# Graph maxima on one core: node positions by a TensorE product, the end mask in the comparison, one register load per group

## The reference

```python
ew = 1.0 / (pos[src] - pos[dst])
def _graph_conv(x, src, dst, ew, W_rel, b_rel, W_root):
    msg = x[src] * ew[:, None]
    agg = jax.ops.segment_max(msg, dst, num_segments=N)
    agg = jnp.where(jnp.isfinite(agg), agg, 0.0)
    return agg @ W_rel.T + b_rel + x @ W_root.T
```

## Time and profile before

| | us |
|---|---|
| median of 3 runs | 5897.64 (5895.26 to 5898.86) |
| profiled execution | 5895.44 |
| its span | 5893.6 |
| preparation (0 to about 191) | 191 |
| maxima stage (about 191 to 1540) | 1349 |

### The profile page before, as it was taken

One profiled execution on the slowest core, in us unless ns is written; L12 is line 12 of the kernel. 1 busy time (PEld: TensorE's weight loads), 2 busy tenths in 40 slices (PEclk: granted clock), 3 DMA queues, 4 the chain that ended last, 5 costly groups with the idle time before them and its releaser, 6 DMA issues. The chain is left out here.

```text
span 5893.6 us, 89741 instructions
## 1 busy us (share of the span) xinstructions
PE 4011.4 (68%) x17170; PEld 2633.9 (45%) x17171; DVE 3584.3 (61%) x11586; ACT 1285.5 (22%) x3616; POOL 2887.2 (49%) x2883
## 2 busy tenths in 40 slices
PE   0466666666577777674997995889998883555531
PEld 0355555555333333332554663555555552444421
DVE  5788888888655655654333115545454546888846
ACT  0243334343222222220000001222222221000020
POOL 1566666666277777772000000577777771333300
PEclk9755555555677777776998996555555555999955
DMA  6466666666312111123886661566666663555520
GB/s 130 148 195 194 195 196 199 200 199 195 103 58 59 51 59 59 51 59 81 200 199 178 193 206 42 157 176 176 176 177 176 176 173 59 142 142 143 142 76 22
DMA packets 1037793, 820.28 MB, mean 139 GB/s; under 512 B 539459, under 2 KB 945586, under 8 KB 1024056
## 3 DMA queue, kind: packets, MB, share of 16 engines
q1 hardware_dynamic: 787472, 600.56, 34.3%
q0 software_dynamic: 98672, 176.74, 11.8%
q10 hardware_dynamic: 151592, 42.33, 3.4%
HBM read 578.48 MB, written 167.05 MB: 126 GB/s over the span
## 5 line engine op out<-in xcount | busy, mean ns | idle before, releaser
L2087 POOL DMA_INDIRECT ring<-xl_rows,idx x896 | 892.5, 996 | 1283.7 <-DVE idx L2166 1009.0
L378 POOL DMA_INDIRECT ringa<-x_sign_pos,idxa x880 | 890.2, 1012 | 434.5 <-issue 275.5
L964 POOL DMA_INDIRECT edge_counts<-cntb,placeb x850 | 844.0, 993 | 349.6 <-issue 257.0
L2159 PE MATMUL zps<-We,eaT 64*128 64x128 f32 x1792 | 710.8, 498 | 0.0
L440 PE MATMUL sela<-hota,endsa 128*128 128x128 f32 x1760 | 404.0, 401 | 335.9 <-ACT endsa L405 314.4
L2157 PE MATMUL zps<-xr,hotT 128*128 x2688 | 454.0, 301 | 145.0 <-ACT hotT L2139 78.4
L2513 PE MATMUL ops<-val,hot 128*128 128x200 f32 x1792 | 364.1, 347 | 263.1 <-DVE out L2532 165.3
L440 PEld LDWEIGHTS sela<-hota,endsa 128*128 128x128 f32 x1760 | 346.2, 293 | 417.2 <-DVE acc L500 318.1
L2189 DVE TENSOR_TENSOR z<-zps,ring 128x512 f32<-128x512 f32 x224 | 154.9, 691 | 604.2 <-PE zps L2159 513.9
L2159 PEld LDWEIGHTS zps<-We,eaT 64*128 64x128 f32 x1792 | 447.3, 309 | 164.6 <-issue 148.2
L2480 POOL TENSOR_TENSOR val<-rows,val 128x512 f32<-128x512 f32 x224 | 235.3, 1050 | 493.4 <-ACT val L2499 493.4
(11 more groups left out here) (337 smaller groups left out, 6245.1 us busy)
## 6 DMA issues: line engine op xcount, KB each, us to landing
edge_counts<-zeroa SPq DMA_DIRECT2D x55, 1568.0 KB
matd<-edge_counts SPq DMA_DIRECT2D x12, 6272.0 KB
posb<-edge_keys SPq DMA_DIRECT2D x50, 1216.0 KB
dstb<-dst_in_tile SPq DMA_DIRECT2D x112, 512.0 KB
xl_of_steps<-ring SPq DMA_DIRECT2D x224, 256.0 KB
rows<-xl_of_steps SPq DMA_DIRECT2D x224, 256.0 KB
reseta<-resets SPq DMA_DIRECT2D x110, 512.0 KB
eaT<-in_eaT SPq DMA_DIRECT2D x896, 32.0 KB
```

What stands on the lines that cost most here:

```text
L378: p.indirect_dma_start(out=ring[:, k, :], out_offset=None, in_=table, in_offset=bass.IndirectOffsetOnAxis(ap=idx[:, k:k + 1], axis=0)).the ...
L964: p.indirect_dma_start(out=g.M.rearrange("d s -> (d s)").unsqueeze(1), out_offset=bass.IndirectOffsetOnAxis(ap=place[:, i, k:k + 1], axis= ...
L2087: p.indirect_dma_start(out=ring[:, c, k, :], out_offset=None, in_=g.xl_rows[0:N, :], in_offset=bass.IndirectOffsetOnAxis(ap=idx[:, q * GS ...
L2159: ins = t.matmul(zk, eaT[:, c, k, :], g.We[:, :], start=False, stop=True)
```

## The change

Four edits, all for `max_pass`.

The positions of the destinations no longer come from four DVE instructions. ACT builds the transposed one-hot matrix `hotT` (nodes on the partitions, edges along the columns) from a bf16 broadcast of the destinations, in two instructions per group, and TensorE multiplies it by the positions of the node tile, split into three bf16 parts, four products of three columns. DVE adds the three parts by one small reduction. `g.posb` goes; `pos3` takes its place. ACT issues the loads of the broadcast row, half a turn at a time.

`g.dend` is the destination where the edge is the last of its destination, and -1 elsewhere; `hot` compares with it, so `ends` is copied without a mask, by one instruction.

DVE loads the node tiles of a group once, after the scan, for the adds of the next step. TensorE has a load of its own. The four adds of DVE now stand together at the start of its step.

`prepare` makes the new tables, and writes the bf16 row to DRAM.

```diff
@@ prepare
+        drel_h = m.sb("drel_h", [P, KB, P], BF16)
+        pos = m.sb("pos_of_nodes", [P, NT])
...
-                s.wait_ge(s_v, V_T + 8)
+                s.wait_ge(s_v, V_T + 13)
...
+                for dst, srct in ((g.d0row, flag[:, :, :]), (g.drelrow, drel_r[:, :, :]), (g.drelhalf, drel_h[:, :, :]),
+                                  (g.srcrow, rows_f[:, :, 0, :])):
...
-                s.dma_start(g.posb[:, 0:N], a["node_vec"].partition_broadcast(P)).then_inc(s_pos, 16)
+                s.dma_start(pos[:, 0:NT - 1], a["node_vec"][0:(NT - 1) * P].rearrange("(t p) -> p t", p=P)).then_inc(s_nodes, 16)
+                s.dma_start(pos[0:N - (NT - 1) * P, NT - 1:NT], a["node_vec"][(NT - 1) * P:N].unsqueeze(1)).then_inc(s_nodes, 16)
...
+                link(v.tensor_copy(drel_h[:, :, :], drel_r[:, :, :]))
+                v.wait_ge(s_nodes, 32)
+                link(v.tensor_copy(g.pos3[:, :, 0], pos[:, :]))
+                link(v.tensor_tensor(pos_rest[:, :], pos[:, :], g.pos3[:, :, 0], ALU.subtract))
+                link(v.tensor_copy(g.pos3[:, :, 1], pos_rest[:, :]))
+                link(v.tensor_tensor(g.pos3[:, :, 2], pos_rest[:, :], g.pos3[:, :, 1], ALU.subtract))
...
+                link(v.scalar_tensor_tensor(out=g.dend[:, :], in0=g.drel[:, :], scalar=1.0, in1=g.endf[:, :],
+                                            op0=ALU.add, op1=ALU.mult))
+                link(v.tensor_scalar(g.dend[:, :], g.dend[:, :], 1.0, None, ALU.subtract))
@@ max_pass, ACT
-                    for k in range(GS):
-                        ins = s.activation(ends[:, q % 2, k, :], runT[q % 2][:, k * P:(k + 1) * P], ACT.Copy,
-                                           scale=g.endf[:, bass.ds(G * GS + k, 1)])
-                    ins.then_inc(s_e, 1)
+                    s.activation(ends[:, q % 2, :, :].rearrange("p k f -> p (k f)"), runT[q % 2][:, :], ACT.Copy
+                                 ).then_inc(s_e, 1)
+
+                def load(turn, h):
+
+                    s.dma_start(dstb[:, h, :], g.drelhalfflat[bass.ds(turn * (U * P) + h * (U * P // 2), U * P // 2)
+                                                              ].partition_broadcast(P)).then_inc(s_b[h], 16)
+
+                def places(turn, G, q):
+
+                    h, off = q // 2, (q % 2) * GS * P
+                    if q % 2 == 0:
+                        s.wait_ge(s_b[h], 16 * (turn + 1))
+                    wait(s, s_hotT, G)
+                    s.activation(apart[:, :], dstb[:, h, off:off + GS * P], ACT.Abs, bias=nodes[:, :]).then_inc(s_apart, 1)
+                    wait(s, s_at, G - 1)
+                    wait(s, s_apart, G + 1)
+                    if q % 2 == 1:
+                        load(turn + 1, h)
+                    s.activation(hotT[:, q % 2, :], apart[:, :], ACT.Relu, scale=-1.0, bias=1.0).then_inc(s_hotT, 1)
...
                 def body(it):
                     for q in range(NG):
                         G = it * NG + q
+                        places(it if q < NG - 1 else it + 1, G + 1, (q + 1) % NG)
@@ max_pass, TensorE
+                def positions(G, q):
+                    t.load(regs, g.T[0:1, bass.ds(G * GS, GS)])
+                    T = [t.snap(r, min_val=0, max_val=NT - 1) for r in regs]
+                    wait(t, s_hotT, G + 1)
+                    wait(t, s_c, (G - 2) * NCH + 1)
+                    for k in range(GS):
+                        ins = t.matmul(where[q % 2][:, 3 * k:3 * k + 3], hotT[:, q % 2, k * P:(k + 1) * P],
+                                       g.pos3.rearrange("p t i -> p (t i)")[:, bass.ds(T[k] * 3, 3)], start=True, stop=True)
+                    ins.then_inc(s_at, 1)
+
                 def body(it):
                     for q in range(NG):
                         G = it * NG + q
+                        positions(G, q)
                         for lag, stage in ((3, select), (1, transposed), (2, back)):
@@ max_pass, DVE step
                     if adds:
-                        A = tiles_of(G - 4, aregs)
-                        add(*at(4), 0, A)
+                        A = [v.snap(r, min_val=0, max_val=NT - 1) for r in aregs]
+                        for k in range(GS):
+                            add(*at(4), k, A)
                     if new:
 
                         wait(v, s_sel, G - NG + 1)
 
                         v.tensor_tensor(hot[:, q, :, :], bc_mid(g.iota_n[:, :], GS),
-                                        bc_last(g.drel[:, bass.ds(G * GS, GS)], P), ALU.is_equal).then_inc(s_hot, 1)
-                        T = tiles_of(G, tregs)
-                        dst_position(G, 0, T)
...
-                        dst_position(G, 3, T)
+                                        bc_last(g.dend[:, bass.ds(G * GS, GS)], P), ALU.is_equal).then_inc(s_hot, 1)
                     if on(2):
                         scan(*at(2), it if q >= 2 else it - 1, ((q - 2) % NG) // 2)
+                    if on(3):
+                        load_tiles(G - 3)
                     if new:
+                        v.wait_ge(s_at, G + 1)
+                        v.tensor_reduce(posd[:, :], where[q % 2][:, 0:3 * GS].rearrange("p (k i) -> p k i", i=3), AX.X, ALU.add
+                                        ).then_inc(s_c, 1)
                         v.wait_ge(s_c, G * NCH + 1)
                         v.wait_ge(s_g[q], 64 * (it + 1))
                         wait(v, s_sg, G - 1)
```

More of the change, by code:

```diff
@@ L136, in prepare @@
         s_pos = m.sem("s_pos")
+        s_nodes = m.sem("s_nodes")
         s_padded = m.sem("s_padded")
@@ L340, in max_pass @@
         sel = [m.bank(f"sel{tag}{i}") for i in range(2)]
+        where = [m.bank(f"where{tag}{i}") for i in range(2)]
         s_idx = m.sem(f"s_idx{tag}")
@@ L344, in max_pass @@
         s_rst = [m.sem(f"s_rst{tag}{i}") for i in range(2)]
+        s_b = [m.sem(f"s_b{tag}{i}") for i in range(2)]
+        s_apart = m.sem(f"s_apart{tag}")
+        s_hotT = m.sem(f"s_hotT{tag}")
+        s_at = m.sem(f"s_at{tag}")
         s_hot = m.sem(f"s_hot{tag}")
@@ L403, in ends_of @@
                     wait(s, s_sel, G - 1)
-                    for k in range(GS):
-                        ins = s.activation(ends[:, q % 2, k, :], runT[q % 2][:, k * P:(k + 1) * P], ACT.Copy,
-                                           scale=g.endf[:, bass.ds(G * GS + k, 1)])
-                    ins.then_inc(s_e, 1)
+                    s.activation(ends[:, q % 2, :, :].rearrange("p k f -> p (k f)"), runT[q % 2][:, :], ACT.Copy
[14 more added lines that the diff above has]
+                    s.activation(hotT[:, q % 2, :], apart[:, :], ACT.Relu, scale=-1.0, bias=1.0).then_inc(s_hotT, 1)
+                load(0, 0)
+                load(0, 1)
+                s.wait_ge(s_ini, 3)
+                places(0, 0, 0)
                 def body(it):
@@ L423, in _ @@
                     ends_of(TURNS * NG - b, NG - b)
+                for h in range(2):
+                    s.wait_ge(s_b[h], 16 * (TURNS + 1))
             @block.tensor
@@ L449, in transposed @@
                     ins.then_inc(s_mT, 1)
+                regs = [t.alloc_register(f"p{tag}{j}") for j in range(GS)]
+                def positions(G, q):
[7 more added lines that the diff above has]
+                    ins.then_inc(s_at, 1)
                 def body(it):
@@ L469, in _ @@
                 v.memset(run[:, :, :], -BIG).then_inc(s_ini, 1)
-                v.wait_ge(s_ini, 2)
+                v.tensor_scalar(nodes[:, :], g.iota_p[:, :], -1.0, None, ALU.mult).then_inc(s_ini, 1)
+                v.wait_ge(s_ini, 3)
                 v.tensor_copy(idx[:, :], g.src_f[:, 0:U]).then_inc(s_idx, 2)
-                tregs = [v.alloc_register(f"t{tag}{j}") for j in range(GS)]
                 def next_indices(it, h):
@@ L478, in _, with load_tiles @@
                 aregs = [v.alloc_register(f"a{tag}{j}") for j in range(GS)]
-                def tiles_of(G, regs):
-                    v.load(regs, g.T[0:1, bass.ds(G * GS, GS)])
-                    return [v.snap(r, min_val=0, max_val=NT - 1) for r in regs]
+                def load_tiles(G):
+                    v.load(aregs, g.T[0:1, bass.ds(G * GS, GS)])
                 def scan(G, q, it_half, h):
@@ L559, in step @@
                             next_indices(it, q // 2)
-                    if adds:
-                        add(*at(4), 3, A)
-                    if new:
                         v.wait_ge(s_c, G * NCH + 2)
@@ new lines, in build @@
+                g.dend = m0.sb("dst_of_ends", [P, KB * P])
+                g.pos3 = m0.sb("pos3", [P, NT, 3], BF16)
+                prepare(nc, g, a)
+                dense_tables(nc, g, a)
+                max_pass(nc, g, "a", g.xp[0:N, :], g.accT, True)
+                all_have_equal(nc, g)
+                lack = nc.values_load(g.lack[0:1, 0:1], min_val=0, max_val=N + 2 * KB * P)
+                with nc.If(lack > 0):
+                    nc.all_engine_barrier()
+                    layer0(nc, g, a, "f", True, False)
```

(14 more changed lines are left out.)

65 lines of the change are left out of this document (15 added, 50 removed).

## The result

The changed kernel takes 5773.0 us (median of 4 runs, 5762.1 to 5777.2), the kernel before beside it 5897.9: a ratio of 0.978, 95% interval 0.977 to 0.980. That is 124.9 us less; the forecast was 134.6 less. The profiled execution took 5762.1 us with a span of 5760.2, against 5895.4 and 5893.6: 133.3 us less. It is the fastest of its four; the other three took 5771.8 to 5777.2.

What follows compares the result with a forecast made beforehand. DVE set the pace before; POOL was to bound the changed loop at 21.7 us a turn. 55 x (24.18 - 21.7) = 136; 5895.4 - 136 + 2 - 1 = 5760, the median 2.2 above: 5763; range 5722 to 5848.

Steps and rivals of the forecast that it cites:

- if a chain I took as hidden ends last: Maxima loop: one of two stated signs that the prediction is wrong; the other was a step period above 5.65 us.
- VectorE's step: Maxima loop on DVE: a new step of 5.16 us, against 5.65 for an unstalled step before.
- The branch: Loop's branch in the maxima stage: given the 0.16 us a turn left over from 24.18.
- POOL sets the pace: Maxima loop after the change: bound by POOL at 21.0 to 22.5 us a turn, 5718 to 5805 us; chance 0.60.
- The term of 0.7 for the long gathers: POOL's gathers: two of 1.31 or 1.32 us a turn, instead of 0.95, bring its floor from 21.0 to 21.7.
- The term 4 x 0.26: POOL's turn: the first gather of each of four groups takes 0.26 us more, idle 0.55 ahead of it.
- Loads over 1 us: none: Register loads on DVE and TensorE: a sign that no load would take over 1 us after the change.
- held until some 3.3 us after the issue: Register loads: held until some 3.3 us after SP issues the clearing of edge_counts, wherever the load stands.
- Rival 1: Maxima loop: the stall stays, in DVE or TensorE's new load; 23.1 us a turn, 5840 us; chance 0.18.
- Rival 2: Maxima loop: products late to the reduction, or TensorE and DVE wait in turns; 22.6 a turn, 5810 us; chance 0.15.
- Rival 4: Slower: the row of destinations lands late and stops ACT, TensorE and DVE; 5957 us at 20 us latency; chance 0.04.
- Preparation and traffic: Before the loop: +2 us (0 to +4); in the loop: 240 GB/s, DMA share about 0.74.

Runs made afterwards that it cites:

- Experiments 3: Changed kernel with VectorE's four adds of a step apart again, using two register sets: 5737.9 us, ratio 0.971 against the kernel before.
- experiment 6: Changed kernel with VectorE's register load put back in front of the first add that uses it: 5870.7 us, ratio 0.995 against the kernel before.
- experiment 2: Kernel before with only the clearing of edge_counts moved, issued behind the first of the turn's two reset loads: 5945.5 us, ratio 1.006.
- experiment 4: Changed kernel with the end mask undone, four masked ScalarE copies in place of one: 5818.7 us, ratio 0.984 against the kernel before.
- experiment 7: Changed kernel with the row of destinations kept in float32, loads of 512 KB instead of 256 KB: 5775.8 us, ratio 0.978 against the kernel before.
- experiments 7 and 9: The second of the two: changed kernel with two first-layer tiles put back where they lay before: 5775.9 us, ratio 0.978; first-layer pass 1120.2 us.

## Why the prediction was right, and where its steps were wrong

The sign, the size and the range held. The turn was forecast at 21.7 and measured at 21.41. But that GpSimd would set the pace, the branch to which most of the chance went, is wrong, and two terms that were wrong met in the number. By the prediction's own sign, "if a chain I took as hidden ends last", its mechanism failed there: VectorE's chain, taken as hidden at 20.8, ends last.

- **VectorE's step** was sized well: 5.16 forecast, 5.13 measured. The chained adds stand 0.43 apart, as the earlier trace rows had it. The reduction takes 0.14 and nd starts 0.18 behind it; `ends` takes 0.60 (0.68 forecast). The list of parts adds up to 5.00, since the add that leaves the stretch before zs stands in it twice; the sum by stretches, 5.16, has it once and is the right one.
- **The branch** was mis-sized. I gave it the 0.16 left over from the earlier trace rows. That step is 0.6 longer here: the idle times of 0.33, 0.23 and 0.21 are in it, less the short gaps that the other steps have there too. VectorE's turn is then 21.2, not 20.8. Part of this could be read in the trace of before, in its step with the branch:

```profile
410.74 0.16 DVE L578 SCALAR_TENSOR_TENSOR w2a<-nda,wna 128x4 f32<-128x4 f32 x1
411.65 0.29 DVE L500 TENSOR_TENSOR acc<-acc,sela 128x128 f32 x1 [0.76 <-issue]
```

  It ends at 416.73, so it is 5.99 long, 0.34 more than the step that I read. The step with the stall is 6.96 (median), 1.3 more and not 1.42. So the stall was priced 0.1 too high in the turn of before, and the branch 0.2 too low.
- **"POOL sets the pace" fell.** The term of 0.7 for the long gathers was right in size: the mean of 991 ns is (0.991 - 0.95) x 16 = 0.66 a turn above 16 of 0.95. It was not two gathers of 1.31, though. The term 4 x 0.26 was wrong. The idle time of 0.55 in the earlier trace rows was not a fixed cost of a group; with the adds apart, and VectorE's messages earlier, it is gone (0.312 ahead of a gather on average, all sixteen places alike). Its floor is 20.7, and VectorE at 21.2 lies above it. Experiments 3 and 6 show it from both sides: less on VectorE and the turn falls to 20.69, more and it rises by 1.73 for some 1.9.
- **The long gathers.** On the rule of the Trainium skill, "SBUF — State Buffer", section "Who interferes with whom": the trace agrees that they collide, but the price is no fixed 0.36. A gather takes longer by what is left of VectorE's instruction, less some 0.12: in the changed kernel 1.38 when it begins 0.1 us into the comparison (30 gathers, medians), 1.19 at 0.3 (11), 1.01 at 0.5 (35), 0.95 at 0.6 (70). 185 of the 880 begin inside it and lose 27.6 us in all; 216 begin inside a message, 0.34 long, and lose 10.6. So collisions are many and mostly cheap, and L515, 0.35 long, showed next to nothing (42 gathers that begin 0.2 into it take 0.96).
- **The stall** went off the path, but not as written. "Loads over 1 us: none" was wrong on both engines. The step that failed is "held until some 3.3 us after the issue": with the clearing moved they were held up to 4.5, in the changed kernel up to 4.3 on VectorE, and in experiment 6 only 1.3 to 1.8. The counts under experiment 2 give what holds in its place. The load was saved by the scan above it, which I had named as the second cover, and on TensorE by the gap before `ends`. TensorE's load was to begin some 3.0 us after the issue and be held 0.3 more; it began 1.4 after it and took 1.8. Rival 1 was thus true in its mechanism (a slow load a turn on TensorE, too) and wrong in its price: 0 instead of 1.4.
- **Rival 2** did not come: TensorE's chain is 4.90 (407.07, the transposes, to 411.97, the end of select; 5.1 forecast), and the products start 1.5 to 1.8 us after the transposes; even in the step with the slow load, 2.4. But the second part of the change carries that: without the mask folded, TensorE would be late, and 34 of the 152 us would be gone (experiment 4).
- **Rival 4** did not come, and experiment 7 puts it far off: with twice the bytes there is still no wait.
- **Preparation and traffic**: +2 forecast, +0 measured (the first scan at 206.4 and 206.3); 240 GB/s and 0.74 forecast, 244 and 0.76 measured.
- **What nothing in the prediction covered** is the first-layer pass, +13. The loop gave 152 where I had 136; the pass behind, and some 6 us in the drain and the later passes, took 19 back.
- **The step from the profiled execution to the median** was put at 2.2, the value of before, and measured 10.9 (5773.0 - 5762.1). Against the profiled execution the forecast of 5760 was 2 off; most of the 10 us of the whole lie in this term.

So the prediction came within 10 us partly by luck: GpSimd's turn was put 1.0 us too high, VectorE's 0.4 too low, which left the larger of the two 0.3 off. What the loop gained beyond the forecast was lost in a pass that the change does not touch.

## What to carry to other kernels

Before a wait is added to an engine's own cost, see whether it shrinks when the other side is early; an idle time in front of the first of a group is a reaction time as long as that engine is the one that waits. A stall that comes from outside need not be removed, only put under an instruction that the engine would run anyway. A remainder of a turn is not to be given to one place before every step of the turn has been read. And after a change to a loop, compare the passes behind it turn by turn: a pass whose turn is in step with the clock's changes lost 13 us here with no computation changed in it, and ten idle instructions ahead of its loop brought it back from 1120 (experiments 7 and 9) to 1103.

## What the runs showed of the chip that I had not expected

- A load of four values from SBUF into registers takes 0.33 to 0.35 us on VectorE and TensorE alike, and up to 1.87 us (TensorE) when it begins 0.7 to 4.4 us after a clearing of 1568 KB has been issued. It isn't let go at a fixed time after that issue: these loads ended 1.3 to 5.4 us after it.
- The same 25 turns differ by up to 2.4 us each with a shift of 0.11 us of one instruction in them. The pass took 1101 to 1105 us in five profiles without the shift and 1115 to 1131 in seven with it. Ten one-column clearings took the pass back to 1103.
- The same edit is worth nothing or much by what stands beside it: the mask alone +8 us, and -34 us in the loop once the position products have left VectorE.
